# Attention in a four-stage graph and mixture kernel: row of maxima through the score banks, a division in four parts, and denominators partly summed by accumulating transfers

## The chip, the cores and the metric

One core of a Trainium2 chip. The metric is device time in microseconds of the whole kernel, launch to end, median of several runs. Times of the profile are from one execution under the hardware profiler.

## The reference

3327 tokens of width 256 go through a graph layer, a mixture of eight experts (top 2), a second graph layer, attention with 8 heads of 32 features, and a second mixture with a capacity. Each result is added to `x`. Only the attention is changed:

```python
h = _layernorm(x, ln1_g, ln1_b)
q = (h @ wq + bq).reshape(B, S, N_HEADS, dk)
...
scores = jnp.einsum('bqhd,bkhd->bhqk', q, k) / np.sqrt(dk)
attn = jax.nn.softmax(scores, axis=-1)
ctx = jnp.einsum('bhqk,bkhd->bqhd', attn, v).reshape(B, S, D)
x = x + ctx @ wo + bo
```

## The kernel before, in words

`attend` works in 26 blocks: two groups of four heads, times 13 chunks of 256 queries. A block has 26 key tiles of 128 keys, taken two at a time in 13 cycles (`CYCLES`). All engines walk the same list of cycles; the cycle within a block is `c`.

- **Scores.** For a key tile, `scores` on TensorE (PE) makes two units, each one PSUM bank of two heads (`ps_s`, three banks in rotation; a unit waits until ScalarE has taken the unit three before). The stack of queries has a row of negated maxima, so the product already has the maximum of each query subtracted. ScalarE (ACT) takes a unit with one exponential into `probs`, a ring of six key tiles.
- **Values and denominators.** `values` multiplies a tile of `probs` with the values into `ps_oz[:, 0]`. The denominator is the sum of the probabilities over all keys: `shares` multiplies by ones into `ps_oz[:, 1]`. So that PE doesn't do this for each tile, GpSimd (POOL) adds up 14 tiles of a block (`POOL_TILES`, 13 additions) into `pool_sum`, and `close` makes one set of shares of it at the start of the next block (cycle 0, after the values of tiles 24 and 25). The other 12 tiles have shares of their own. ACT may write a slot of the ring only when PE and POOL are through with it (lines 1184 to 1187).
- **Maxima.** One to two blocks ahead, `run` makes plain scores into `ps_x`, four banks in two pairs, one pair per job, two jobs per cycle; VectorE (DVE) reduces each pair to maxima (L1219, L1222). The job in pair `u % 2` waits until job `u - 2` has been taken. When a block's maxima are complete, a `row` job (cycle 9, L1148) turns them into a row, in the same pair rotation, and ACT writes that row, negated, into the query stack (L1201). At cycle 0 `close` is followed on ACT by the evacuation of `ps_oz` (L1208); at cycle 1 DVE divides (L1239, L1241); at cycle 4 an `out` job multiplies by `wo` (L1153) in the pair rotation, and DVE adds it to `x` (L1228).

The order of a cycle on PE is: both units of tile 2c, the first of tile 2c+1, the jobs, the second unit of tile 2c+1, then the values of tiles 2c-2 and 2c-1 (at cycle 0: tiles 24 and 25 of the block before, then `close`). Every engine runs its instructions in order. Plain loads are on the SP queue; POOL issues no DMA in this stage.

Of the kernel before, what the change touches and what calls it, by code (L numbers as in the profile page):

```python
# [9 lines left out]
ALU = mybir.AluOpType  # L10
# [945 lines left out]
RING = 6  # L956
POOL_TILES = [i * 23 // 13 for i in range(14)]
POOL_ADDS = len(POOL_TILES) - 1
CYCLES = NT // 2
BLOCKS = HG * NCH  # L960
MAX_AHEAD, ROW_AT, DIVIDE_AT, OUT_AT = 19, 9, 1, 4
K_PIECES = [(0, 7), (7, 14), (14, 20), (20, NT)]


def attention_jobs():


    jobs = {}
    count = 0
    full = [("max", qt, hp, kc) for kc in range(NP // KEYS) for qt in range(QT) for hp in range(2)]  # L970
    full += [("tail", 0, hp, NP // KEYS) for hp in range(2)]
    for cycle in range(-MAX_AHEAD, BLOCKS * CYCLES + OUT_AT + 1):
        now = []
        ahead, j = divmod(cycle + MAX_AHEAD, CYCLES)
        if ahead < BLOCKS:
            now += [(kind, ahead, qt, hp, kc) for kind, qt, hp, kc in full[2 * j:2 * j + 2]]
        g, c = divmod(cycle, CYCLES)
        if c == ROW_AT and 0 <= g + 1 < BLOCKS:
            now.append(("row", g + 1, 0, 0, 0))
# [4 lines left out]
    return jobs  # L984


def attend(nc, m, t, s):
# [4 lines left out]
    last_max = {job[2]: job[0] for job in flat if job[1] == "tail"}  # L992
    freed_by_act = [sum(job[1] == "row" for job in flat[:n + 1]) for n in range(len(flat))]
    UNITS = 2 * NT
    S_BANKS = 3
# [4 lines left out]
    ones_row = s("ones_row")  # L1000
    scored, exped, used = s("scored"), s("exped"), s("probs_used")
    x_made, x_free, max_made, rows_made = s("x_made"), s("x_free"), s("max_made"), s("rows_made")
    pool_added, summed, evacuated, context = s("pool_added"), s("summed"), s("evacuated"), s("context")
    with ExitStack() as ctx:
# [8 lines left out]
        probs, wo = sb("probs", [P, RING, FOUR, CHUNK]), sb("wo", [P, HG, D])  # L1013
        pool_sum = sb("pool_sum", [P, 2, FOUR, CHUNK])
        part_max, maxima = sb("part_max", [P, 2, FOUR, QT, NP // KEYS + 1]), sb("maxima", [P, FOUR * QT], BF16)
# [7 lines left out]
        def _(sp):  # L1023
# [15 lines left out]
            def load_query_stack(g):  # L1039
                hg, b = divmod(g, NCH)  # L1040
                if g >= 2:
                    sp.wait_ge(scored, (g - 1) * UNITS)
# [14 lines left out]
            for g in range(2, BLOCKS):  # L1057
# [3 lines left out]
                if g == NCH:  # L1061
                    for piece, (_, end) in enumerate(K_PIECES):
                        if piece == 2:
                            load_queries(g + 2)
                        sp.wait_ge(scored, (NCH - 1) * UNITS + 2 * end)
                        load_stack(1, piece)

        @block.gpsimd
        def _(pool):
            pool.memset(kst[STACK:STACK + 1].bitcast(F32), 1.0).then_inc(ones_row, 1)  # L1070
            for g in range(BLOCKS):
                for n, k in enumerate(POOL_TILES[1:], 1):
                    tile = g * NT + k
                    pool.wait_ge(exped, 2 * tile + 2)
                    if n == 1:
# [9 lines left out]
        def _(pe):  # L1085
            def scores(g, k, halves):
# [4 lines left out]
                for j in halves:  # L1091
                    unit = (g * NT + k) * 2 + j
                    if unit >= S_BANKS:
                        pe.wait_ge(exped, unit - S_BANKS + 1)
                    for hh in range(2):
# [10 lines left out]
            def values(g, k):  # L1106
                hg, tile = g // NCH, g * NT + k
                rows = LAST if k == NT - 1 else P
                pe.wait_ge(exped, 2 * tile + 2)
# [12 lines left out]

            def run(job):
                u, kind, g, qt, hp, kc = job
                pair = u % 2 * 2
                if u >= 2 and flat[u - 2][1] == "row":
                    pe.wait_ge(rows_made, freed_by_act[u - 2])
                elif u >= 2:
                    pe.wait_ge(x_free, u - 1 - freed_by_act[u - 2])
                if kind == "max":  # L1130
# [7 lines left out]
                elif kind == "tail":  # L1138
                    for q in range(QT):
                        for hh in range(2):  # L1140
                            at = slice((2 * hp + hh) * DK, (2 * hp + hh + 1) * DK)
                            last = pe.matmul(ps_x[:, pair + hh, q * CHUNK:q * CHUNK + NP - kc * KEYS], queries[at, g % 2, q * P:(q + 1) * P],
                                             keys[at, g // NCH, kc * KEYS:NP], start=True, stop=True)
                elif kind == "row":
                    pe.wait_ge(max_made, g + 1)
                    for h in range(FOUR):
                        for q in range(QT):
                            last = pe.matmul(ps_x[STACK:STACK + 1, pair + h // 2, h % 2 * CHUNK + q * P:h % 2 * CHUNK + (q + 1) * P],  # L1148
                                             maxima[:, h * QT + q:h * QT + q + 1], m.ident_b[:], start=True, stop=True)
                else:  # L1150
                    pe.wait_ge(context, 2 * (g + 1))
                    for q in range(QT):
                        last = pe.matmul(ps_x[:, pair + q, 0:D], cx[:, q * P:(q + 1) * P], wo[:, g // NCH, :], start=True, stop=True)  # L1153
                last.then_inc(x_made, 1)

            pe.wait_ge(ones_row, 1)
            pe.wait_ge(wo_loaded, 16)
            for cycle in sorted(jobs):
                g, c = divmod(cycle, CYCLES)
                if 0 <= g < BLOCKS:  # L1160
                    if c == 0:
                        pe.wait_ge(q_loaded[g % 2], g // 2 * 48 + 48)
                        pe.wait_ge(rows_made, g + 1)
                    scores(g, 2 * c, (0, 1))
                    scores(g, 2 * c + 1, (0,))
                for job in jobs[cycle]:
                    run(job)
                if 0 <= g < BLOCKS:
# [5 lines left out]
                elif g >= 1:  # L1174
                    values(g - 1, NT - 2)
                    values(g - 1, NT - 1)
                    close(g - 1)

        @block.scalar
        def _(act):  # L1180
            def exponentials(g, k):
                tile = g * NT + k
                if tile >= RING:
                    act.wait_ge(used, tile - RING + 1)
                    before, kb = divmod(tile - RING, NT)
                    if kb in POOL_TILES:
                        act.wait_ge(pool_added, before * POOL_ADDS + max(1, POOL_TILES.index(kb)))
                for j in range(2):
                    act.wait_ge(scored, 2 * tile + j + 1)
                    act.activation(probs[:, tile % RING, 2 * j:2 * j + 2], ps_s[:, (2 * tile + j) % S_BANKS], ACT.Exp,  # L1190
                                   scale=scale).then_inc(exped, 1)

            for cycle in sorted(jobs):
                g, c = divmod(cycle, CYCLES)
                if 0 <= g < BLOCKS:
                    exponentials(g, 2 * c)
                    exponentials(g, 2 * c + 1)
                for u, kind, block_of, *_ in jobs[cycle]:
                    if kind == "row":
                        act.wait_ge(x_made, u + 1)  # L1200
                        act.activation(qst[STACK:STACK + 1, block_of % 2, :, :].rearrange("p h n -> p (h n)"),  # L1201
                                       ps_x[STACK:STACK + 1, u % 2 * 2:u % 2 * 2 + 2, :].rearrange("p a n -> p (a n)"),
                                       ACT.Copy, scale=-1.0).then_inc(rows_made, 1)
                if g >= 1 and c == 0:
                    act.wait_ge(summed, g)
                    if g >= 2:
                        act.wait_ge(context, 2 * (g - 1))
                    act.activation(oz[:], ps_oz[:], ACT.Copy).then_inc(evacuated, 1)  # L1208

        @block.vector  # L1210
        def _(dve):
            def take(job):
# [7 lines left out]
                elif kind == "tail":  # L1220
                    both = ps_x[:, pair, :].rearrange("p a (q n) -> p a q n", q=QT)
                    dve.tensor_reduce(part_max[:, g % 2, heads, :, kc], both[:, :, :, 0:TOKENS - kc * KEYS], AX.X, ALU.max).then_inc(x_free, 1)  # L1222
                    if hp == 1:
                        dve.wait_ge(x_free, u + 1 - freed_by_act[u])
                        dve.tensor_reduce(maxima[:], part_max[:, g % 2].rearrange("p h q k -> p (h q) k"), AX.X, ALU.max).then_inc(max_made, 1)
# [4 lines left out]
            for cycle in sorted(jobs):  # L1230
                g, c = divmod(cycle, CYCLES)
                for job in jobs[cycle]:
                    if job[1] != "row":
                        take(job)
                if g >= 1 and c == DIVIDE_AT:
                    dve.wait_ge(evacuated, g)
                    if g >= 2:
                        dve.wait_ge(context, 2 * g - 2)
                    dve.reciprocal(rden[:], oz[:, 1, :]).then_inc(context, 1)  # L1239
                    dve.wait_ge(context, 2 * g - 1)  # L1240
                    dve.tensor_tensor(cx[:], oz[:, 0, :], rden[:], ALU.mult).then_inc(context, 1)  # L1241
            dve.wait_ge(x_free, len(flat) - freed_by_act[-1])

# [160 lines left out]
```

## Time and profile before

| what | us |
|---|---|
| median of 3 runs (3333.06 to 3336.5) | 3336.18 |
| the profiled execution's own time | 3331.71 |
| its span, first to last instruction | 3330.0 |
| PE busy over the span | 2526.9 (76%) |
| DVE busy | 2022.8 (61%) |
| ACT busy | 1520.0 (46%) |
| POOL busy | 1058.5 (32%) |

The attention blocks fill 1578 to 2842 us of the span. A row of a timeline merges neighbouring instructions of one line; its first number is the start, its second the stretch to the end of the last of them, and in brackets is the idle time ahead with the instruction that ended it.

### The profile page before, as it was taken

The numbers are of one execution on the slowest core, as the hardware profiler recorded it, in microseconds if no ns is written. First come the engines' busy times: TensorE is split into PE (matmuls) and PEld (weight loads), VectorE is DVE, ScalarE is ACT, GpSimd is POOL, SyncE is SP. The second block draws the span as 40 slices with busy tenths as digits, with TensorE's granted clock in tenths as the row PEclk, the third lists the DMA queues.
The fourth block names the chain that finished last, engine by engine and source line by source line (L and its number), as shares of the span: only waits on it lengthen the run. The fifth ranks groups of instructions, "written<-read, shape, count | busy, mean of one in ns | idle before, by whom it ended". The sixth has DMA issues, their size and how long they took to land. (4 is left out here: it accounts for less than half of the span.)

```text
span 3330.0 us, 54843 instructions
## 1 busy us (share of the span) xinstructions
PE 2526.9 (76%) x21272; PEld 1929.4 (58%) x21272; DVE 2022.8 (61%) x2670; ACT 1520.0 (46%) x2591; POOL 1058.5 (32%) x596
## 2 busy tenths in 40 slices
PE   0399732888891699494999999999999999317883
PEld 0388632888881588481555555555555555317883
DVE  7944522777773644545667666666666663426773
ACT  0233312666660433250656556555655556205661
POOL 0100023000005000011666666666665666230003
PEclk9999956999995899795999999999999999658997
DMA  9865204555542654254000000030000000115552
GB/s 410 360 218 175 68 33 157 213 199 210 219 172 84 239 169 161 84 163 122 9 12 14 9 14 13 14 71 12 14 9 13 14 8 6 41 41 221 208 217 99
DMA packets 140109, 375.97 MB, mean 113 GB/s; under 512 B 22032, under 2 KB 82704, under 8 KB 121872
## 3 DMA queue, kind: packets, MB, share of 16 engines
q1 hardware_dynamic: 122928, 319.82, 27.3%
q0 software_dynamic: 15696, 48.77, 4.1%
q10 hardware_dynamic: 1296, 4.75, 0.4%
q8 instruction: 132, 2.16, 0.3%
q14 instruction: 57, 0.47, 0.0%
HBM read 314.30 MB, written 58.98 MB: 112 GB/s over the span
## 5 line engine op out<-in xcount | busy, mean ns | idle before, releaser
L1219 DVE TENSOR_REDUCE at_part_max<-ps_x 128x2 f32<-128x1024 f32 x624 | 731.4, 1219 | 391.3 <-PE ps_x L1136 391.3
L1190 ACT ACTIVATE at_probs<-ps_s 128x512 f32<-128x512 f32 x1352 | 706.1, 603 | 482.0 <-PE ps_s L1096 481.3
L1082 POOL TENSOR_TENSOR at_pool_sum<-at_pool_sum,at_probs 128x1024 f32<-128x1024 f32 x312 | 746.8, 2394 | 347.0 <-ACT at_probs L1190 335.8
L1096 PE MATMUL ps_s<-at_qst,at_kst 97*128 97x256 f32 x2704 | 515.9, 314 | 5.2 <-ACT at_probs L1190 5.1
L1096 PEld LDWEIGHTS ps_s<-at_qst,at_kst 97*128 97x128 f32 x2704 | 375.3, 194 | 224.6 <-issue 128.5
L461 PE MATMUL ps_acc<-adj_hi,y_hi 128*128 128x512 f32 (+1 forms) x728 | 280.1, 385 | 230.7 <-DVE adj_lo L508 230.7
L1113 PE MATMUL ps_oz<-at_probs,k_xhat 128*32 128x256 f32 (+1 forms) x5408 | 419.7, 401 | 0.0
L508 DVE TENSOR_TENSOR adj_lo<-adj_raw,adj_hi 128x1024 fp32r<-128x1024 f32 (+1 forms) x182 | 207.4, 1147 | 241.0 <-ACT adj_hi L430 241.0
L430 ACT ACTIVATE adj_hi<-adj_raw 128x1024 fp32r<-128x1024 f32 (+1 forms) x182 | 181.9, 999 | 305.4 <-PE ps_acc L463 289.1
L732 PE MATMUL ps_ex_o<-ex_w_hi,ex_hid_hi 128*128 128x256 f32 x864 | 245.7, 284 | 75.9 <-DVE ex_hid_lo L811 69.5
L461 PEld LDWEIGHTS ps_acc<-adj_hi,y_hi 128*128 128x128 f32 x728 | 138.2, 190 | 258.8 <-issue 230.8
L462 PE MATMUL ps_acc<-adj_lo,y_hi 128*128 128x512 f32 (+1 forms) x728 | 277.1, 381 | 0.0
L463 PE MATMUL ps_acc<-adj_hi,y_lo 128*128 128x512 f32 (+1 forms) x728 | 277.1, 381 | 0.0
L781 ACT ACTIVATE ex_hid<-ps_ex_h,ex_b 128x256 f32<-128x256 f32 x432 | 197.1, 474 | 166.4 <-PE ps_ex_h L734 139.4
L830 POOL DMA_DIRECT2D results<-ex_res x54 | 38.7, 717 | 723.8 <-DVE ex_res L817 723.8
L799 DVE TENSOR_TENSOR ex_w_lo<-ex_w,ex_w_hi 128x2048 fp32r<-128x2048 f32 x108 | 242.7, 2289 | 33.8 <-ACT ex_w_hi L771 33.8
L732 PE MATMUL ps_ex_h<-ex_rt_hi,ex_w_hi 128*128 128x256 f32 x864 | 243.9, 282 | 9.8 <-DVE ex_w_lo L799 9.8
L1136 PE MATMUL ps_x<-at_keys,at_queries 32*128 32x512 f32 x1248 | 197.1, 513 | 68.1 <-DMA at_wo<-wo 40.6
L734 PE MATMUL ps_ex_h<-ex_rt_hi,ex_w_lo 128*128 128x256 f32 x864 | 241.5, 280 | 0.0
L733 PE MATMUL ps_ex_h<-ex_rt_lo,ex_w_hi 128*128 128x256 f32 x864 | 241.4, 279 | 0.0
L734 PE MATMUL ps_ex_o<-ex_w_hi,ex_hid_lo 128*128 128x256 f32 x864 | 240.4, 278 | 0.0
L733 PE MATMUL ps_ex_o<-ex_w_lo,ex_hid_hi 128*128 128x256 f32 x864 | 240.4, 278 | 0.0
(181 smaller groups left out, 3960.3 us busy)
## 6 DMA issues: line engine op xcount, KB each, us to landing
ex_w<-w SPq DMA_DIRECT2D x108, 1024.0 KB, 6.7
adj_raw<-adjT SPq DMA_DIRECT2D x156, 512.0 KB, 4.0
adj_rows<-adj SPq DMA_DIRECT2D x26, 1664.0 KB, 10.7
slots<-zeros POOLq DMA_DIRECT2D x27, 512.0 KB, 21.5
ex_rows<-slots SPq DMA_DIRECT2D x54, 256.0 KB, 2.9
results<-ex_res POOLq DMA_DIRECT2D x54, 256.0 KB, 2.7
at_qst<-qk_parts SPq DMA_DIRECT2D x78, 128.0 KB, 2.5
ex_b<-b SPq DMA_DIRECT2D x54, 128.0 KB, 2.1
```

Source lines behind the costliest of these rows:

```text
L461: pe.matmul(out, y_hi[:, k, cols], hi[:, g % PIECE_RING, at], start=k == 0, stop=False)
L462: pe.matmul(out, y_hi[:, k, cols], lo[:, g % PIECE_RING, at], start=False, stop=False)
L463: last = pe.matmul(out, y_lo[:, k, cols], hi[:, g % PIECE_RING, at], start=False, stop=k == NT - 1)
L732: pe.matmul(out, hi, by_hi, start=start, stop=False)
L733: pe.matmul(out, hi, by_lo, start=False, stop=False)
L734: return pe.matmul(out, lo, by_hi, start=False, stop=stop)
L799: dve.tensor_tensor(w_lo[:, k, layer, :], w[:, k, layer, :], w_hi[:, k, layer, :].bitcast(F32), ALU.subtract).then_inc(weights_lo, 1)
L1082: pool.tensor_tensor(pool_sum[:, g % 2], pool_sum[:, g % 2], probs[:, tile % RING], ALU.add).then_inc(pool_added, 1)
L1096: last = pe.matmul(ps_s[:, unit % S_BANKS, hh, :], kst[:, 2 * j + hh, k * P:(k + 1) * P], qst[:, g % 2, 2 * j + hh, :], start=True, stop=True)
L1113: last = pe.matmul(ps_oz[h * DK:(h + 1) * DK, 0, :], m.xhat[0:rows, k, (hg * FOUR + h) * DK:(hg * FOUR + h + 1) * DK], probs[0:rows, tile ...
L1190: act.activation(probs[:, tile % RING, 2 * j:2 * j + 2], ps_s[:, (2 * tile + j) % S_BANKS], ACT.Exp, scale=scale).then_inc(exped, 1)
L1219: dve.tensor_reduce(part_max[:, g % 2, heads, qt, kc], ps_x[:, pair, :], AX.X, ALU.max).then_inc(x_free, 1)
```

## The change

The row of maxima no longer takes a pair of `ps_x`. It takes two units of the score banks, at cycle 10, at the end of the cycle on PE; ACT writes the row in two halves. The numbers of units come from `score_units`. The `out` job moves to the end of cycle 6. The division is done in four parts of 64 queries at cycles 1 to 4. The maxima start 17 cycles ahead, not 19. Of a block's key tiles, 14 go to POOL's additions (13 as before), 8 are added into `dma_sum` by DMAs that POOL issues, each after the one before has landed (the first is a plain copy), and 4 (8, 17, 24, 25) keep shares of their own on PE. `close` makes shares of both sums.

```diff
-POOL_TILES = [i * 23 // 13 for i in range(14)]
+SUM_TILES = [k for k in range(NT - 2) if k not in (8, 17)]
+DMA_TILES = [2, 5, 9, 12, 15, 19, 21, 23]
+POOL_TILES = [k for k in SUM_TILES if k not in DMA_TILES]
-MAX_AHEAD, ROW_AT, DIVIDE_AT, OUT_AT = 19, 9, 1, 4
+MAX_AHEAD, ROW_AT, DIVIDE_AT, DIVIDE_PARTS, OUT_AT = 17, 10, 1, 4, 6
...
+            def send(g, k):
+                n, tile = DMA_TILES.index(k), g * NT + k
+                before = g * len(DMA_TILES) + n
+                pool.wait_ge(taken, tile_unit[tile] + 2)
+                if n == 0 and g >= 2:
+                    pool.wait_ge(summed, g - 1)
+                if before:
+                    pool.wait_ge(dma_added, 16 * before)
+                if n == 0:
+                    pool.dma_start(dma_sum[:, g % 2], probs[:, tile % RING]).then_inc(dma_added, 16)
+                else:
+                    pool.dma_start(dma_sum[:, g % 2], probs[:, tile % RING], accum_op=ALU.add).then_inc(dma_added, 16)
...
-                for n, k in enumerate(POOL_TILES[1:], 1):
+                for k in SUM_TILES[1:]:
+                    if k in DMA_TILES:
+                        send(g, k)
+                        continue
...
-                if k not in POOL_TILES:
+                if k not in SUM_TILES:
                     last = shares(probs[:, tile % RING], rows, False)
...
                 pe.wait_ge(pool_added, (g + 1) * POOL_ADDS)
-                shares(pool_sum[:, g % 2], P, True).then_inc(summed, 1)
+                shares(pool_sum[:, g % 2], P, False)
+                pe.wait_ge(dma_added, 16 * len(DMA_TILES) * (g + 1))
+                shares(dma_sum[:, g % 2], P, True).then_inc(summed, 1)
...
+            def row(g):
+                pe.wait_ge(max_made, g + 1)
+                for half in range(2):
+                    unit = row_unit[g] + half
+                    if unit >= S_BANKS:
+                        pe.wait_ge(taken, unit - S_BANKS + 1)
+                    for hh in range(2):
+                        for q in range(QT):
+                            col = (2 * half + hh) * QT + q
+                            last = pe.matmul(ps_s[STACK:STACK + 1, unit % S_BANKS, hh, q * P:(q + 1) * P],
+                                             maxima[:, col:col + 1], m.ident_b[:], start=True, stop=True)
+                    last.then_inc(scored, 1)
...
+                for job in jobs[cycle]:
+                    if job[1] == "out":
+                        run(job)
+                if c == ROW_AT and 0 <= g + 1 < BLOCKS:
+                    row(g + 1)
...
+                    if kb in DMA_TILES:
+                        act.wait_ge(dma_added, 16 * (before * len(DMA_TILES) + DMA_TILES.index(kb) + 1))
...
-                if g >= 1 and c == DIVIDE_AT:
+                if g >= 1 and DIVIDE_AT <= c < DIVIDE_AT + DIVIDE_PARTS:
+                    done = 2 * (DIVIDE_PARTS * (g - 1) + c - DIVIDE_AT)
+                    at = slice((c - DIVIDE_AT) * CHUNK // DIVIDE_PARTS, (c - DIVIDE_AT + 1) * CHUNK // DIVIDE_PARTS)
                     dve.wait_ge(evacuated, g)
...
+                    dve.reciprocal(rden[:, at], oz[:, 1, at]).then_inc(context, 1)
+                    dve.wait_ge(context, done + 1)
+                    dve.tensor_tensor(cx[:, at], oz[:, 0, at], rden[:, at], ALU.mult).then_inc(context, 1)
```

## Rows read from the trace of the kernel before

**Rows 1.** Windows: us from to, length, busy per engine (instructions), PEclk, DMA share, GB/s

```profile
core 0: us, PE busy (x) PEld busy (x) DVE busy (x) ACT busy (x) POOL busy (x), PEclk, DMA share, GB/s
1628.10:2842.10 1214.00, 1135.63 (x12000) 688.40 (x12000) 788.70 (x709) 713.61 (x1345) 776.27 (x325) 0.96 0.06 15
2119.80:2167.00 47.20, 44.08 (x485) 26.97 (x485) 33.43 (x30) 28.67 (x54) 31.09 (x14) 1.00 0.04 13
2069.20:2119.80 50.60, 47.39 (x485) 28.59 (x486) 33.43 (x30) 28.69 (x54) 31.04 (x14) 0.93 0.04 12
2083.00:2086.00 3.00, 3.00 (x21) 1.70 (x23) 1.07 (x2) 0.60 (x1) 0.77 (x1) 0.50 0.00 0
```

**Rows 2.** PE timeline, one block: cycles without and with shares, and three stalls

```profile
2019.24 0.61 PE L1102 MATMUL ps_oz<-at_probs,k_ones 127*32 127x256 f32 x8
2019.67 0.62 PE L1102 MATMUL ps_oz<-at_pool_sum,k_ones 128*32 128x256 f32 x8
2020.21 0.98 PE L1096 MATMUL ps_s<-at_qst,at_kst 97*128 97x256 f32 x6
...
2022.99 0.98 PE L1096 MATMUL ps_s<-at_qst,at_kst 97*128 97x256 f32 x6
...
2028.46 0.50 PE L1136 MATMUL ps_x<-at_keys,at_queries 32*128 32x512 f32 x2 [0.63 <-DVE at_part_max L1219]
...
2033.48 1.13 PE L1153 MATMUL ps_x<-at_wo,at_cx 128*128 128x256 f32 x4 [1.32 <-DVE at_part_max L1219]
2034.27 0.59 PE L1096 MATMUL ps_s<-at_qst,at_kst 97*128 97x256 f32 x2
...
2051.35 0.61 PE L1148 MATMUL ps_x<-k_ident_b,at_maxima 128*1 128x128 bf16 x8 [1.14 <-DVE at_part_max L1219]
```

**Rows 3.** DVE timeline, division of the same block and a plain cycle

```profile
2023.94 1.74 DVE L1239 RECIPROCAL at_rden<-at_oz 128x256 f32<-128x256 f32 x1
2025.71 0.42 DVE L1241 TENSOR_TENSOR at_cx<-at_oz,at_rden 128x256 f32<-128x256 f32 x1
...
2050.07 2.36 DVE L1219 TENSOR_REDUCE at_part_max<-ps_x 128x2 f32<-128x1024 f32 x2 [0.41 <-PE ps_x L1136]
```

**Rows 4.** Timeline after the last block: small divisions and products on DVE

```profile
2858.43 0.32 DVE L206 RECIPROCAL bn_rs<-bn_rs 128x26 f32<-128x26 f32 x1 [0.29 <-ACT bn_rs L270]
2858.78 0.19 DVE L207 TENSOR_TENSOR bn_nb<-bn_rs 128x26 f32<-128x26 f32 x1
```

**Rows 5.** Groups of POOL, line engine op: count, busy us, mean ns, idle before

```profile
L1082 POOL TENSOR_TENSOR at_pool_sum<-at_pool_sum,at_probs 128x1024 f32<-128x1024 f32 x312 | 746.8, 2394 | 347.0 <-ACT at_probs L1190 335.8 <-POOL at_pool_sum L1082 0.5
L830 POOL DMA_DIRECT2D results<-ex_res x54 | 38.7, 717 | 723.8 <-DVE ex_res L817 723.8
L400 POOL DMA_DIRECT2D slots<-zeros x27 | 14.6, 553 | 0.6 <-POOL zeros L393 0.6
```

**Rows 6.** POOL timeline: five additions in a row, and two DMA issues in a row

```profile
2823.26 12.45 POOL L1082 TENSOR_TENSOR at_pool_sum<-at_pool_sum,at_probs 128x1024 f32<-128x1024 f32 x5 [0.76 <-ACT at_probs L1190]
...
3287.53 0.95 POOL L849 DMA_INDIRECT got<-results,mx_get  x1 [0.30 <-issue]
3288.78 0.95 POOL L849 DMA_INDIRECT got<-results,mx_get  x1 [0.30 <-issue]
```

**Rows 7.** DMA issues: queue and count, KB each, median us from issue to landing

```profile
slots<-zeros POOLq DMA_DIRECT2D x27, 512.0 KB, 21.5
results<-ex_res POOLq DMA_DIRECT2D x54, 256.0 KB, 2.7
x_kept<-k_x SPq DMA_DIRECT2D x1, 3328.0 KB, 9.3
slots<-k_xhat,mx_put POOLq DMA_INDIRECT x78, 2.4
```

**Rows 8.** PE timeline ahead of the first block: two successive maxima jobs

```profile
1540.19 0.79 PE L1136 MATMUL ps_x<-at_keys,at_queries 32*128 32x512 f32 x2 [0.34 <-DVE at_part_max L1219]
1541.32 0.79 PE L1136 MATMUL ps_x<-at_keys,at_queries 32*128 32x512 f32 x2 [0.34 <-DVE at_part_max L1219]
```

More of the change, by code:

```diff
@@ L977, in attention_jobs @@
         g, c = divmod(cycle, CYCLES)
-        if c == ROW_AT and 0 <= g + 1 < BLOCKS:
-            now.append(("row", g + 1, 0, 0, 0))
         if c == OUT_AT and g >= 1:
@@ L984, in attention_jobs, with score_units @@
     return jobs
+def score_units():
+    tile_unit, row_unit, n = {}, {}, 0
+    for cycle in range(-CYCLES, BLOCKS * CYCLES):
+        g, c = divmod(cycle, CYCLES)
+        if g >= 0:
+            for k in (2 * c, 2 * c + 1):
+                tile_unit[g * NT + k] = n
+                n += 2
+        if c == ROW_AT and g + 1 < BLOCKS:
+            row_unit[g + 1] = n
+            n += 2
+    return tile_unit, row_unit
 def attend(nc, m, t, s):
@@ L992, in attend @@
     last_max = {job[2]: job[0] for job in flat if job[1] == "tail"}
-    freed_by_act = [sum(job[1] == "row" for job in flat[:n + 1]) for n in range(len(flat))]
-    UNITS = 2 * NT
+    tile_unit, row_unit = score_units()
     S_BANKS = 3
@@ L1000, in attend @@
     ones_row = s("ones_row")
-    scored, exped, used = s("scored"), s("exped"), s("probs_used")
-    x_made, x_free, max_made, rows_made = s("x_made"), s("x_free"), s("max_made"), s("rows_made")
+    scored, taken, used = s("scored"), s("scores_taken"), s("probs_used")
+    x_made, x_free, max_made = s("x_made"), s("x_free"), s("max_made")
+    dma_added = s("dma_added")
     pool_added, summed, evacuated, context = s("pool_added"), s("summed"), s("evacuated"), s("context")
@@ L1041, in load_query_stack @@
                 if g >= 2:
-                    sp.wait_ge(scored, (g - 1) * UNITS)
+                    sp.wait_ge(scored, tile_unit[(g - 1) * NT - 1] + 2)
                 for r, part in enumerate((0, 1, 0)):
@@ L1064, in _ @@
                             load_queries(g + 2)
-                        sp.wait_ge(scored, (NCH - 1) * UNITS + 2 * end)
+                        sp.wait_ge(scored, tile_unit[(NCH - 1) * NT + end - 1] + 2)
                         load_stack(1, piece)
@@ L1070, in _ @@
             pool.memset(kst[STACK:STACK + 1].bitcast(F32), 1.0).then_inc(ones_row, 1)
-            for g in range(BLOCKS):
-                for n, k in enumerate(POOL_TILES[1:], 1):
-                    tile = g * NT + k
-                    pool.wait_ge(exped, 2 * tile + 2)
+            def send(g, k):
[10 more added lines that the diff above has]
+                    pool.dma_start(dma_sum[:, g % 2], probs[:, tile % RING], accum_op=ALU.add).then_inc(dma_added, 16)
+            for g in range(BLOCKS):
+                for k in SUM_TILES[1:]:
+                    if k in DMA_TILES:
+                        send(g, k)
+                        continue
+                    n, tile = POOL_TILES.index(k), g * NT + k
+                    pool.wait_ge(taken, tile_unit[tile] + 2)
                     if n == 1:
@@ L1091, in scores @@
                 for j in halves:
-                    unit = (g * NT + k) * 2 + j
+                    unit = tile_unit[g * NT + k] + j
                     if unit >= S_BANKS:
-                        pe.wait_ge(exped, unit - S_BANKS + 1)
+                        pe.wait_ge(taken, unit - S_BANKS + 1)
                     for hh in range(2):
@@ L1108, in values @@
                 rows = LAST if k == NT - 1 else P
-                pe.wait_ge(exped, 2 * tile + 2)
+                pe.wait_ge(taken, tile_unit[tile] + 2)
                 if k == 0 and g:
@@ L1125, in run @@
                 pair = u % 2 * 2
[L1126 to L1129, printed above, removed]
+                if u >= 2:
+                    pe.wait_ge(x_free, u - 1)
                 if kind == "max":
@@ L1143, in run @@
                                              keys[at, g // NCH, kc * KEYS:NP], start=True, stop=True)
[L1144 to L1149, printed above, removed]
                 else:
-                    pe.wait_ge(context, 2 * (g + 1))
+                    pe.wait_ge(context, 2 * DIVIDE_PARTS * (g + 1))
                     for q in range(QT):
@@ L1162, in _ @@
                         pe.wait_ge(q_loaded[g % 2], g // 2 * 48 + 48)
-                        pe.wait_ge(rows_made, g + 1)
+                        pe.wait_ge(taken, row_unit[g] + 2)
                     scores(g, 2 * c, (0, 1))
@@ L1166, in _ @@
                 for job in jobs[cycle]:
-                    run(job)
+                    if job[1] != "out":
+                        run(job)
                 if 0 <= g < BLOCKS:
@@ L1177, in _ @@
                     close(g - 1)
+                for job in jobs[cycle]:
+                    if job[1] == "out":
+                        run(job)
+                if c == ROW_AT and 0 <= g + 1 < BLOCKS:
+                    row(g + 1)
         @block.scalar
@@ L1187, in exponentials @@
                         act.wait_ge(pool_added, before * POOL_ADDS + max(1, POOL_TILES.index(kb)))
+                    if kb in DMA_TILES:
+                        act.wait_ge(dma_added, 16 * (before * len(DMA_TILES) + DMA_TILES.index(kb) + 1))
                 for j in range(2):
-                    act.wait_ge(scored, 2 * tile + j + 1)
-                    act.activation(probs[:, tile % RING, 2 * j:2 * j + 2], ps_s[:, (2 * tile + j) % S_BANKS], ACT.Exp,
-                                   scale=scale).then_inc(exped, 1)
+                    unit = tile_unit[tile] + j
+                    act.wait_ge(scored, unit + 1)
+                    act.activation(probs[:, tile % RING, 2 * j:2 * j + 2], ps_s[:, unit % S_BANKS], ACT.Exp,
+                                   scale=scale).then_inc(taken, 1)
             for cycle in sorted(jobs):
@@ L1197, in _ @@
                     exponentials(g, 2 * c + 1)
[L1198 to L1203, printed above, removed]
+                if c == ROW_AT and 0 <= g + 1 < BLOCKS:
+                    for half in range(2):
+                        unit = row_unit[g + 1] + half
+                        act.wait_ge(scored, unit + 1)
+                        act.activation(qst[STACK:STACK + 1, (g + 1) % 2, 2 * half:2 * half + 2, :],
+                                       ps_s[STACK:STACK + 1, unit % S_BANKS], ACT.Copy, scale=-1.0).then_inc(taken, 1)
                 if g >= 1 and c == 0:
@@ L1206, in _ @@
                     if g >= 2:
-                        act.wait_ge(context, 2 * (g - 1))
+                        act.wait_ge(context, 2 * DIVIDE_PARTS * (g - 1))
                     act.activation(oz[:], ps_oz[:], ACT.Copy).then_inc(evacuated, 1)
@@ L1223, in take @@
                     if hp == 1:
-                        dve.wait_ge(x_free, u + 1 - freed_by_act[u])
+                        dve.wait_ge(x_free, u + 1)
                         dve.tensor_reduce(maxima[:], part_max[:, g % 2].rearrange("p h q k -> p (h q) k"), AX.X, ALU.max).then_inc(max_made, 1)
@@ L1232, in _ @@
                 for job in jobs[cycle]:
-                    if job[1] != "row":
-                        take(job)
-                if g >= 1 and c == DIVIDE_AT:
+                    take(job)
+                if g >= 1 and DIVIDE_AT <= c < DIVIDE_AT + DIVIDE_PARTS:
+                    done = 2 * (DIVIDE_PARTS * (g - 1) + c - DIVIDE_AT)
+                    at = slice((c - DIVIDE_AT) * CHUNK // DIVIDE_PARTS, (c - DIVIDE_AT + 1) * CHUNK // DIVIDE_PARTS)
                     dve.wait_ge(evacuated, g)
[L1237 to L1242, printed above, removed]
+                    if done:
+                        dve.wait_ge(context, done)
+                    dve.reciprocal(rden[:, at], oz[:, 1, at]).then_inc(context, 1)
+                    dve.wait_ge(context, done + 1)
+                    dve.tensor_tensor(cx[:, at], oz[:, 0, at], rden[:, at], ALU.mult).then_inc(context, 1)
+            dve.wait_ge(x_free, len(flat))
 def attention(nc, m, t, s):
```

3 lines of the change are left out of this document (2 added, 1 removed).

## The prediction, made blind

> **What bounds the kernel now.** I read the windows of the attention stage first, then one block on each engine, then what POOL and its DMAs cost elsewhere in the kernel, because the trace has no DMA on POOL in this stage. The 25 intervals between block ends take 1214 us, so 48.56 us a block [rows 1]. PE is busy 94% of that, DVE 65%, ACT 59%, POOL 64%: PE sets the pace. In the PE timeline of a block [rows 2] the reader should see two things. A cycle without shares is 2.78 us (2020.21 to 2022.99) and one set of shares is 0.43 (2019.24 to 2019.67). And three times a block PE stands still for DVE: 0.63 us after the division, 1.32 ahead of the `out` job, 1.14 ahead of the `row` job, the last two because a third job in a cycle needs a pair that DVE is still reducing. After such a stall the granted clock sometimes falls to 0.50, that is 1.2 GHz, as at 2083 us; a block without that takes 47.2 us, one with it twice 50.6, so a fall costs 1.7 us [rows 1].
>
> **PE's own work after the change.** Plain cycles: 13 x 2.78 = 36.1 us. Sets of shares: before 12 + 1 = 13, after 4 + 2 = 6, so 6 x 0.43 = 2.6 us (3.0 less). The row is 0.54 and `out` 0.79 us (2033.48 to 2034.27); both are only moved. Their stalls of 1.14 and 1.32 go: at the end of the cycle DVE has had some 2 us for the pair, and the row needs no pair. Late next would be a score bank for the row, which waits for exponentials issued over 1 us before: nothing. The `out` result is added by DVE during the next cycle's first scores, a 0.7 us piece under 0.9 us of cover; without the cover it would be a stall of up to 0.7.
>
> **The division in parts** removes little. A reciprocal of 256 columns takes 1.74 us [rows 3], one of 26 takes 0.32 [rows 4]; interpolated, 64 columns take 0.56, and the product 0.23. Four parts of 0.8 us are 3.2 us where one was 2.2. In a plain cycle DVE idles 0.41 us [rows 3], so four cycles with 0.8 each leave it 1.6 behind, less 0.4 of slack: a PE stall of about 1.2 a block (bounds 0 and 1.6), against 0.63 seen plus the hand-overs around it. I take no gain. PE and DVE by themselves would then allow 36.1 + 2.6 + 0.5 + 0.8 + 1.2 = 41.2 us a block.
>
> **POOL and its chain of DMAs** are what I expect to be late next. POOL keeps 13 additions; in a row they come every 2.49 us (12.45 / 5 [rows 6]). It gets 8 issues. Their price: the generation of a DMA of 256 KB took 0.72 us, that of the 512 KB of zeros 0.55 [rows 5]; then 0.30 until the next instruction [rows 6]. An accumulating one must also name its second source, so I take the upper, 1.02 each (bounds 0.55, as if the gap were hidden, and 1.25, the pitch of the indirect ones). Work alone is 13 x 2.49 + 8 x 1.02 = 40.5 us, as much as PE's.
>
> To that come landings. Each send waits for the one before to have landed, and it stands in POOL's queue, so the additions behind it wait as well. Call issue to landing L. Between the sends of tiles 2, 5, 9, 12, 15 and 19 lie two additions each (1.02 + 4.98 = 6.0 us), which hide an L up to 5.7. Between 19, 21 and 23 lies one, 1.02 + 2.49 = 3.5 us, so there POOL waits L + 0.3 each. After 23, `close` on PE waits for the landing, and all of the next block's tiles but 0 and 1 are queued behind it on PE, and on ACT behind the evacuation that `close` releases. POOL has only the addition of tile 1 to do meanwhile. So one block runs, from landing to landing:
> - `close`'s second shares 0.43, scores of tile 2 0.91, exponential 0.60, three hand-overs of about 0.1: 2.3 us until send 2;
> - five sends (2, 5, 9, 12, 15): 5.1 us; ten additions: 24.9 us. PE makes the 17 tiles from 2 to 19 in some 24 us, so POOL doesn't run dry;
> - sends 19, 21, 23: 3 L + 0.6.
>
> Together 32.9 + 3 L. The ring doesn't add to it: the slots of tiles 20 to 23 are asked for by tiles 0 to 3 of the next block, late in the same order.
>
> **L.** No row shows an accumulate. The nearest is the 256 KB from POOL, 2.7 us, beside 2.4 for the 128 KB of the indirect one: 0.3 per 128 KB, so 3.3 for a plain 512 KB [rows 7]. The accumulate reads 512 KB more: at (9.3 - 2.7) / (3328 - 256) us per KB, 1.1 us. That makes 4.4. Low end: 3.3, the second read for nothing. High end by the rows: 21.5, the zeros, but those were queued behind each other and large loads, so I count them as evidence for a tail only; a chain of reads and writes that don't overlap, twice the 0.6 + 1.1 of data time, gives 6.1. I take 4.4.
>
> The Trainium skill (DMA: Bandwidth & Descriptors, Anatomy of one DMA) fits a DMA from GpSimd as about 2.0 us plus bytes at 436 GB/s; by it a plain 512 KB is an estimated 3.2 us. Its page Collectives: The Full Stack (Part 3) says that a reduce is held back by its two reads and not by the addition, which would make an estimated 4.4; if the addition and second read were free, the chain below would be that of the first rival. No row here shows either.
>
> **The clock.** PE now stalls in `close` for some 5 us a block, longer than any stall of before. The mean block has (48.56 - 47.2) / 1.7 = 0.8 falls for its two long stalls [rows 1], so one follows roughly every second stall. It would lie on the chain's first piece; I take half of one, 0.85 (bounds 0 and 1.7).
>
> **The sum.** 32.9 + 13.2 + 0.85 = 46.95 us a block against 48.56: -1.6 x 26 = -42 us. Ahead of the first block, DVE paces maxima at 1.13 us a job [rows 8]; two cycles less are four jobs, -4.5. At the end the last division in four dependent parts costs +1.1. Together -45. The profiled execution took 3331.7 us (span 3330.0), 4.5 below the median; against the median, 3336.2 - 45 = 3291.
>
> **Rivals.**
> 1. The transfers are hidden, L near 3.3. The chain is 32.9 + 9.9 = 42.8, PE and DVE allow 41.2, and the freed stalls and shares show almost fully: -5.8 to -7.4 a block, -150 to -195 us, 3141 to 3186; with an issue cheaper by 0.2 the middle between this and my forecast. For it: DMA engines are 6% used in the stage [rows 1]. Against it: a dependent accumulate must read and write the same bytes. 0.25.
> 2. **Slower**: the wait in `close` and at sends 21 and 23. It decides from 32.9 + 3 L = 48.6, so L = 5.2 without a fall of the clock and 4.9 with half a one; each us of L above costs 78 us. L = 5.5 with a fall each block: 51.1, +66 us, 3399. Beyond 5.7 all seven gaps wait: L = 7 gives 2.3 + 7 x 7.3 + 7 = 60.4 us, +310. For it: POOL's own work is already 40.5 us with no landing in it, and the trace says nothing of accumulates. 0.30.
> 3. The row and `out` don't come free as they seem, since DVE after four parts of division is still behind at cycle 6; PE stalls there again by up to 1.3. Under the chain above this is hidden (POOL is the one behind); it only lifts rival 1 from 41.2 to 42.5. Within its figures.
> 4. The parts cancel: what shares and stalls give, 3.0 + 2.5 us, is eaten by the chain within 0.2%. About 0.06.
>
> **How the numbers follow.** The forecast, a chain with L between 3.7 and 4.9, has 0.39: 44.0 to 48.4 a block, 3215 to 3329. Rival 1 0.25, rival 2 0.30, no change 0.06. A measurement of this kernel tells some 0.2%, 7 us. Faster 0.64, same 0.06, slower 0.30. The range leaves out the better half of rival 1 and the far part of rival 2 (L above 5.5): 3165 to 3390.
>
> **What would show it.** Right: intervals between evacuations (L1208 before) near 47 us; POOL's idle time released by landings at tiles 21 and 23, about 1 us each; PE idle some 5 us in `close`, released by a DMA; no idle time of PE ahead of row and `out`; L of the accumulates 4 to 5 us; issues 0.7 us. Wrong: PE idle in `close` near nothing (L or the issue cheaper, rival 1); POOL waiting at all seven gaps (rival 2); DVE ending most of PE's idle time (rival 3). The steps least sure are L, which the sum multiplies by three, and the price of an issue, by five.

## The result and the profile after

The changed kernel takes 3430.5 us in the median of four runs (3398.1 to 3440.6) against 3336.1: a ratio of 1.027, with a 95% interval of 1.020 to 1.034. It is slower, by 94 us where I forecast 45 us faster, and outside my range. Its profiled execution has a span of 3424.8 us.

The first view is again the windows of the stage, here from the first evacuation of `ps_oz` to the last (us from to, length, busy time of PE, weight loads, DVE, ACT and POOL with instructions, granted clock, DMA share, GB/s); then one block in pieces.

```profile
1630.20:2934.20 1304.00, 1176.53 (x10608) 703.86 (x10608) 870.70 (x863) 719.39 (x1370) 931.04 (x524) 0.86 0.44 95
2032.40:2035.80 3.40, 0.80 (x18) 0.23 (x11) 0.43 (x1) 0.00 (x0) 2.15 (x1) 1.00 0.78 154
2038.00:2051.00 13.00, 13.00 (x78) 7.20 (x79) 10.02 (x12) 5.50 (x11) 9.62 (x6) 0.50 0.31 82
2051.00:2072.00 21.00, 21.00 (x214) 13.24 (x217) 17.77 (x18) 14.26 (x28) 18.44 (x11) 0.99 0.41 83
```

The 25 intervals are 52.16 us each, not 48.56 [rows 1] and not the 46.95 forecast. PE has 1392 matmul records less and yet more busy time: the granted clock of the stage is 0.86, where it was 0.96. The third row is what I had not reckoned with. After PE's wait of 2.6 us in `close` the clock stays at 0.50 (1.2 GHz) for 13 us, with PE busy throughout. In the kernel before, the trace has 27 stretches of low clock in the stage and each is 3.4 us long (the one of [rows 1] is among them). In the changed kernel it has 25 between the first and the last evacuation, 3.4 to 27.3 us long, and together they last 345 us, 13.8 us a block. Each of them begins in a wait of PE or at most 2.1 us after it, 23 of them at the wait in `close`.

The waits of the same stretch (engine line, waited for: us in total, times, longest):

```profile
ACT at_oz L1256 <- PE ps_oz L1134: 134.9, 26, 10.0
POOL at_dma_sum L1096 <- ACT at_probs L1238: 110.5, 25, 5.7
PE ps_oz L1134 <- DMA at_dma_sum<-at_probs: 102.6, 25, 11.1
POOL at_pool_sum L1114 <- ACT at_probs L1238: 94.2, 109, 2.1
POOL at_dma_sum L1098 <- DMA at_dma_sum<-at_probs: 81.4, 34, 7.7
POOL at_dma_sum L1098 <- ACT at_probs L1238: 66.1, 37, 4.2
PE ps_x L1168 <- DVE at_part_max L1267: 16.1, 19, 1.8
```

PE waits 102.6 / 25 = 4.1 us a block for the landing in `close`, and the waits at the `row` and `out` jobs [rows 2] are gone. But POOL, which the forecast had busy from tile 2 to tile 19, waits for ACT a further 94.2 + 66.1 us, 6.4 a block: PE at half clock delivers tiles too slowly. One block on POOL shows it:

```profile
2038.38 0.58 POOL L1096 DMA_DIRECT2D at_dma_sum<-at_probs  x1 [3.82 <-ACT at_probs L1238]
...
2044.69 0.85 POOL L1098 DMA_DIRECT2D at_dma_sum<-at_probs  x1
2047.32 4.87 POOL L1114 TENSOR_TENSOR at_pool_sum<-at_pool_sum,at_probs 128x1024 f32<-128x1024 f32 x2 [1.78 <-ACT at_probs L1238]
2053.41 0.87 POOL L1098 DMA_DIRECT2D at_dma_sum<-at_probs  x1 [1.22 <-ACT at_probs L1238]
...
2076.45 0.86 POOL L1098 DMA_DIRECT2D at_dma_sum<-at_probs  x1 [1.73 <-DMA at_dma_sum<-at_probs]
...
2081.95 0.86 POOL L1098 DMA_DIRECT2D at_dma_sum<-at_probs  x1 [2.23 <-DMA at_dma_sum<-at_probs]
```

The move of the `row` job is not quite free. The scores behind it, which otherwise take 0.98 us, take 0.53 more; the weight loads of scores wait for ACT's writes of the row (44 waits, 9.2 us, between 1640 and 2800 us).

```profile
2072.82 1.51 PE L1128 MATMUL ps_s<-at_qst,at_kst 97*128 97x256 f32 x6
```

The transfers themselves, over the whole kernel (queue, count, KB each, median us from issue to landing):

```profile
at_dma_sum<-at_probs POOLq DMA_DIRECT2D x208, 512.0 KB, 4.4
```

L is 4.4 us in the median, the value taken; for the transfer of tile 21 the median is 5.2. An issue is 0.86 us; an addition right behind it starts some 0.6 us after the issue began and takes 2.7 us where others take 2.4, so the pair is as long as both one after the other.

### The profile page after: what moved, and what is told of

The parts are those of the page before. It is cut to its first block and busy times, and to the rows that moved or that the text cites. A ratio compares the mean times of both kernels' runs of the same rounds, so it can differ in the third digit from the quotient of the medians.

```text
span 3424.8 us, 52605 instructions
## 1 busy us (share of the span) xinstructions
PE 2568.9 (75%) x19816; PEld 1946.3 (57%) x19816; DVE 2101.6 (61%) x2826; ACT 1525.3 (45%) x2617; POOL 1220.8 (36%) x804
## 5 line engine op out<-in xcount | busy, mean ns | idle before, releaser
L1114 POOL TENSOR_TENSOR at_pool_sum<-at_pool_sum,at_probs 128x1024 f32<-128x1024 f32 x312 | 768.8, 2464 | 111.5 <-ACT at_probs L1238 97.4
L1128 PE MATMUL ps_s<-at_qst,at_kst 97*128 97x256 f32 x2704 | 582.7, 341 | 6.5 <-ACT at_probs L1238 5.6
L1128 PEld LDWEIGHTS ps_s<-at_qst,at_kst 97*128 97x128 f32 x2704 | 422.2, 216 | 261.0 <-ACT at_probs L1238 137.6
L1145 PE MATMUL ps_oz<-at_probs,k_xhat 128*32 128x256 f32 (+1 forms) x5408 | 428.0, 433 | 0.7 <-ACT at_probs L1238 0.7
L1168 PE MATMUL ps_x<-at_keys,at_queries 32*128 32x512 f32 x1248 | 215.5, 568 | 68.2 <-DMA at_wo<-wo 41.1
```

Of the source, the lines that this page charges most:

```text
L1114: pool.tensor_tensor(pool_sum[:, g % 2], pool_sum[:, g % 2], probs[:, tile % RING], ALU.add).then_inc(pool_added, 1)
L1128: last = pe.matmul(ps_s[:, unit % S_BANKS, hh, :], kst[:, 2 * j + hh, k * P:(k + 1) * P], qst[:, g % 2, 2 * j + hh, :], start=True, stop=True)
```

## The experiments

**Parts alone.** The first takes the transfers out of the change:

```diff
-SUM_TILES = [k for k in range(NT - 2) if k not in (8, 17)]
-DMA_TILES = [2, 5, 9, 12, 15, 19, 21, 23]
+SUM_TILES = [i * 23 // 13 for i in range(14)]
+DMA_TILES = []
...
-                shares(pool_sum[:, g % 2], P, False)
-                pe.wait_ge(dma_added, 16 * len(DMA_TILES) * (g + 1))
-                shares(dma_sum[:, g % 2], P, True).then_inc(summed, 1)
+                shares(pool_sum[:, g % 2], P, True).then_inc(summed, 1)
```

> The change without its transfers: 14 tiles to POOL and shares of their own for 12 tiles on PE, as before; the row in the score banks, the four-part division, the later out and the 17 cycles are kept. Theory (the chain through the landings and the clock that falls after the wait in close make the change slow): PE sets the pace, 13 x 2.78 + 13 x 0.43 + 0.54 + 0.79 + up to 1.2 = 43 to 44.3 us a block at a granted clock near 1.00, so about 110 to 145 us less than before, 3190 to 3225. Rival (the moved row and the division in parts, with products on DVE that stand still beside POOL, are what costs): no faster than before, 3330 or more.

3223.7 us, ratio 0.965 (0.964 to 0.967). The block is 44.31 us at a clock of 1.00, and the first evacuation comes 4.3 us earlier than before (1623.8 against 1628.1): the two cycles less. Its window of the stage:

```profile
1623.80:2731.50 1107.70, 1102.37 (x12008) 677.83 (x12008) 837.66 (x863) 709.85 (x1369) 771.91 (x325) 1.00 0.07 17
```

The second puts the change's `send`, tile lists and two-part `close` alone into the kernel before.

> The kernel before with the transfers alone: 8 tiles by accumulating transfers, 4 by shares, 14 by POOL; row, out and division as before. Theory: the chain of POOL and landings sets the block as in the change, so 50 to 54 us a block, 3380 to 3470, with PE waiting for a landing in close 3 to 5 us a block and the clock low after it; the stalls at row and out are hidden. Rival (the transfers only hurt together with the moved row and division): the shares removed show, 3.0 us a block, 3260 to 3330.

3470.7 us, ratio 1.041 (1.035 to 1.048), a block of 53.27. The slowness is the transfers'; the rest of the change is worth 115 us without them, and 40 beside them. One part of the expectation failed: PE's waits at `row` and `out` are not hidden, they are 26.6 and 30.9 us in the stage. Only 1 of this kernel's 26 products of the division takes longer than 0.43 us, so it is slow without the second cause that is found below.

**The landing's duration.** `accum_op=ALU.add` is removed, nothing else:

> The change with all eight transfers as plain copies into dma_sum, so the denominators leave seven tiles out; each still waits for the one before. A landing then takes 2.9 us instead of 4.5 and an issue 0.58 instead of 0.86. Theory: the chain is 3 x 1.6 + 6 x 0.28 = 6.5 us shorter, the wait in close is near nothing and the clock doesn't fall: 41 to 44 us a block, 3140 to 3220. Rival (the duration of a transfer matters little, it is the order of POOL): 3400 or more.

3309.0 us, ratio 0.992 (0.990 to 0.995), a block of 47.42: 121 us faster than the change, but 3.4 us a block, 89 us in all, above what the theory allowed. The waits in `close` are nearly gone, and still the clock falls (0.94 in the stage). The waits of PE in that stage name another stall (same columns as the list of waits above):

```profile
PE ps_x L1168 <- DVE at_part_max L1267: 60.1, 72, 1.5
PE ps_oz L1134 <- DMA at_dma_sum<-at_probs: 9.9, 2, 9.5
```

**The wait filled with work.**

```diff
                 shares(pool_sum[:, g % 2], P, False)
+                for _ in range(10):
+                    shares(pool_sum[:, g % 2], P, False, nought)
                 pe.wait_ge(dma_added, 16 * len(DMA_TILES) * (g + 1))
```

> The change with ten sets of shares by weights of zero (4.3 us of products that add nothing to the sums) between the shares of pool_sum and the wait for the last landing. Theory (the 4 us wait costs mainly through the 13 us of half clock that follow it): the clock stays near 1.00, the block falls from 52.2 to 46 to 48 us, the time to 3270 to 3320, although PE has 4.3 us of work more. Rival (the landings and POOL's order alone make 52 us, whatever PE's clock): no change or longer, 3420 to 3450.

3461.5 us, ratio 1.037 (1.035 to 1.040), block 53.24: the expectation failed. The clock is low for 191 us in the stage instead of 345, so it did not stay near 1.00. It hardly falls after `close` any more; 22 of its 26 falls come some 13 us later, after another stall. In the timelines of DVE, POOL and PE of this kernel:

```profile
2052.83 0.54 DVE L1294 RECIPROCAL at_rden<-at_oz 128x64 f32<-128x64 f32 x1
2053.40 2.98 DVE L1296 TENSOR_TENSOR at_cx<-at_oz,at_rden 128x64 f32<-128x64 f32 x1
2056.30 2.34 DVE L1273 TENSOR_REDUCE at_part_max<-ps_x 128x2 f32<-128x1024 f32 x2
```

```profile
2053.02 0.85 POOL L1101 DMA_DIRECT2D at_dma_sum<-at_probs  x1
2053.62 5.15 POOL L1117 TENSOR_TENSOR at_pool_sum<-at_pool_sum,at_probs 128x1024 f32<-128x1024 f32 x2
```

```profile
2054.82 0.98 PE L1131 MATMUL ps_s<-at_qst,at_kst 97*128 97x256 f32 x6
2057.57 0.50 PE L1173 MATMUL ps_x<-at_keys,at_queries 32*128 32x512 f32 x2 [1.77 <-DVE at_part_max L1273]
2058.70 0.80 PE L1173 MATMUL ps_x<-at_keys,at_queries 32*128 32x512 f32 x2 [0.63 <-DVE at_part_max L1273]
2059.42 0.80 PE L1131 MATMUL ps_s<-at_qst,at_kst 97*128 97x256 f32 x2
```

The product of 64 columns, 0.22 us alone, takes 2.98: it ends when POOL's first addition does. A product with both operands in SBUF does not get through while POOL is adding. In the trace of the changed kernel 53 of the 104 products are held up; each of them ends 0.08 to 0.09 us after an addition does, and none of the other 51 lies wholly inside one. In the filled kernel DVE falls behind, PE stands 1.77 + 0.63 us for it, and its matmuls then take 0.80 us where they took 0.50. The filler moved the clock's fall from one stall to the next; what it saved in low clock is outweighed by its own 4.3 us a block and by PE's waits for DVE.

**The product left out, alone and with the filler.** The context is written by the reciprocal:

```diff
-                    dve.reciprocal(rden[:, at], oz[:, 1, at]).then_inc(context, 1)
-                    dve.wait_ge(context, done + 1)
-                    dve.tensor_tensor(cx[:, at], oz[:, 0, at], rden[:, at], ALU.mult).then_inc(context, 1)
+                    dve.reciprocal(cx[:, at], oz[:, 1, at]).then_inc(context, 2)
```

> The change with the four products of a block's division left out: the reciprocal alone is written to the context, so the output leaves out the multiplication by the values' sums. The wait in close stays. Theory (two causes of a low clock: the wait in close, and DVE's product held up by POOL's additions): one of two is gone, but the wait in close is still there with its 13 us of half clock; 50 to 52.5 us a block, 3375 to 3430. Rival (the products are the main cost): 46 to 48 us, 3270 to 3320.

3411.6 us, ratio 1.023 (1.020 to 1.026), block 51.45: as expected, the wait in `close` is enough by itself.

> Both at once: ten sets of shares by zero weights ahead of the wait in close, and the products of the division left out. Theory (the chain of POOL and landings costs 46 to 47 us a block once PE's clock stays up; all beyond it in the change is the clock, which falls after either stall): granted clock 0.98 or more, 46 to 47.5 us a block, 3265 to 3310. Rival (each stall costs its own length and the clock is beside the point; or POOL's order alone makes 52 us): 3400 or more, as with either alone.

3329.1 us, ratio 0.997 (0.996 to 0.998), mean block 48.36. So the filler costs 31 us alone, the missing products bring 19 alone, and both together bring 101: one stall of either kind suffices to lower the clock. The two kernels without products differ in the filler alone. With 4.3 us more work for PE in each block, the filled one is 82 us faster, at a clock of 0.98 in the stage instead of 0.87 (the wait alone, then the wait filled):

```profile
1629.20:2915.40 1286.20, 1156.12 (x10608) 695.25 (x10608) 790.69 (x763) 719.67 (x1370) 931.76 (x524) 0.87 0.45 96
1634.80:2843.90 1209.10, 1161.59 (x12608) 709.33 (x12607) 790.01 (x763) 713.70 (x1370) 934.39 (x524) 0.98 0.48 102
```

Time and mean are above what was expected; 15 of the 25 intervals are between 46.7 and 47.3. One such block, with 4.3 us of filler in it:

```profile
2009.54:2056.20 46.66, 45.85 (x509) 28.21 (x510) 33.29 (x32) 28.62 (x56) 37.43 (x21) 1.00 0.48 103
```

and its chain on POOL, where 46.66 us go by from one first send to the next:

```profile
2011.42 0.58 POOL L1099 DMA_DIRECT2D at_dma_sum<-at_probs  x1 [3.87 <-ACT at_probs L1244]
...
2039.96 0.85 POOL L1101 DMA_DIRECT2D at_dma_sum<-at_probs  x1
...
2044.98 0.86 POOL L1101 DMA_DIRECT2D at_dma_sum<-at_probs  x1 [1.77 <-ACT at_probs L1244]
...
2050.96 0.86 POOL L1101 DMA_DIRECT2D at_dma_sum<-at_probs  x1 [2.70 <-DMA at_dma_sum<-at_probs]
...
2058.08 0.58 POOL L1099 DMA_DIRECT2D at_dma_sum<-at_probs  x1 [3.87 <-ACT at_probs L1244]
```

The twelfth interval is 63.1 us; in it the second group's keys are loaded, and a landing took up to 10.5 us in this kernel. The same interval is long in the change (63.8) and with plain copies (57.9), and like the others (44.5) without transfers. That is once 10 to 16 us, which the forecast had not. Of the last five intervals, 47.5 to 54.8 us, one of 50.1 has landings of 6.4 and 6.7 us and ends in a wait of 1.9 us in `close`, and the longest, behind it, begins with 20.5 us of low clock; why those landings are late stays open.

**Plain copies and no products**, both edits above:

> All eight transfers as plain copies, and the products left out (the denominators leave out seven tiles). Theory: neither the wait in close (a landing takes 2.9 us) nor the products stall PE, the clock stays up and PE's own work shows, 41 to 42.5 us a block, 3135 to 3180. Rival (POOL's 13 additions and eight issues bound it by themselves): 45 us or more, 3240 and up.

3183.8 us, ratio 0.953 (0.952 to 0.955); 17 of 25 intervals are 41.3 to 42.0 us, beside the 41.2 that the forecast gave PE and DVE, with one of 54.0 at the keys, one of 52.1 with some 25 us of low clock in it, and a mean of 42.74. The total is just above the expected span for that. One of the short blocks:

```profile
2009.00:2050.30 41.30, 41.28 (x436) 25.67 (x432) 33.25 (x33) 28.37 (x56) 35.13 (x22) 1.00 0.31 116
```

**Fewer transfers.** Four, early, around POOL's tiles of before:

```diff
+SUM_TILES = sorted([i * 23 // 13 for i in range(14)] + [2, 6, 11, 16])
+DMA_TILES = [2, 6, 11, 16]
```

> The change without its late transfers: POOL's 14 tiles as in the kernel before, and only tiles 2, 6, 11 and 16 by transfers, three or more additions apart from the next and the last one long before close; eight tiles keep shares of their own. Theory (a transfer is harmless where its landing is waited for by nobody): PE has four sets of shares less and one more than the kernel without transfers, 3 x 0.43 = 1.3 us less a block, so 43.0 against 44.3 us, 3185 to 3200. Rival (POOL, busier by four issues, holds DVE's products longer, PE stalls for DVE and the clock falls): 3224 or more.

3295.1 us, ratio 0.987 (0.985 to 0.988), block 47.22: the rival, slower than without transfers by 71 us, though nobody waits for a landing. The products took up to 2.44 us and PE waited for DVE 71 times (43.3 us). The same kernel with the products left out:

> The kernel with transfers of tiles 2, 6, 11 and 16, with the four products of the division left out (the output leaves out that multiplication). Theory (a DVE product with both operands in SBUF stands still while POOL adds, DVE falls behind, PE stalls for it and the clock falls; four issues on POOL make that more frequent): without products PE has no stall, the clock is 1.00 and the block is 42.5 to 43.5 us instead of 47.2, 3175 to 3205. Rival (the issues or the transfers themselves slow PE or ACT): 3260 to 3300, as with the products.

3190.4 us, ratio 0.955 (0.954 to 0.957), a block of 42.90 at a clock of 1.00. So 105 us of that kernel, 4.3 a block, hang on four products of a fifth of a microsecond a block. PE's waits for DVE are 1.7 us of them, and the low clock (85 us in that stage, so half of that is lost) another 1.7; the remaining 0.9 is not accounted for.

```profile
1628.20:2700.60 1072.40, 1065.36 (x11408) 660.65 (x11408) 790.28 (x763) 707.22 (x1369) 847.96 (x425) 1.00 0.28 66
```

The division in one part, in the kernel without transfers (`DIVIDE_PARTS` 1):

> The kernel without transfers (row in the score banks, later out) with the division in one part at cycle 1, as before. Theory: the stall of 0.6 us and its hand-overs after the division come back once a block, and the clock seldom falls for it alone: 44.3 to 45.5 us a block, 3222 to 3255. Rival (four products beside POOL cost more than one, 2 us held up at worst each): faster than 3222.

3248.1 us, ratio 0.973 (0.971 to 0.974), block 45.21: four parts are worth 24 us there, more than the nothing I gave them.

**Versions that beat both.** With the division's cycles kept free of transfers:

```diff
-SUM_TILES = [k for k in range(NT - 2) if k not in (8, 17)]
-DMA_TILES = [2, 5, 9, 12, 15, 19, 21, 23]
+SUM_TILES = sorted([i * 23 // 13 for i in range(14)] + [11, 16, 20])
+DMA_TILES = [11, 16, 20]
```

> POOL's 14 tiles as in the kernel before, and transfers of tiles 11, 16 and 20 alone, after the division's cycles (tiles 2 to 9) and with landings that nobody waits for; nine tiles keep shares of their own. Theory: the products meet POOL no more than without transfers, PE saves two sets of shares, 0.9 us a block, 43.4 against 44.3 us: 3195 to 3210. Rival (any transfer on POOL costs more than the shares it saves): 3224 or more.

3209.6 us, ratio 0.962 (0.960 to 0.964), block 43.61: just inside the expected span, with 0.7 us of the 0.9 a block.

```diff
-DMA_TILES = [2, 5, 9, 12, 15, 19, 21, 23]
+DMA_TILES = [10, 13, 16, 19]
+SUM_TILES = sorted([0, 1, 3, 5, 7, 8, 11, 12, 14, 15, 17, 18, 20, 22] + DMA_TILES)
```

> Transfers of tiles 10, 13, 16 and 19, POOL's 14 tiles placed around them with two additions between transfers. Theory: three sets of shares less on PE, 1.3 us, 43.0 us a block, 3185 to 3200, if POOL, some 3.5 us late at tile 22, is through before close; otherwise, and by the rival (POOL's lateness reaches close or the next block's products), PE stalls and the clock falls: 3224 to 3300.

3207.1 us, ratio 0.961 (0.959 to 0.962), block 43.60: 7 us above the expected span. Neither version leaves anything out. The second is 131 us faster than the kernel before, measured beside it, and 223 faster than the changed one; it gets 0.7 of its 1.3 us a block. Most of that is the moved row, the later `out` and the division in parts; the transfers bring 14 to 17 us.

## Why the prediction was wrong

- **The term that failed is the clock**: "It would lie on the chain's first piece; I take half of one, 0.85 (bounds 0 and 1.7)" was the step. In the change the clock is low for 13.8 us a block, in stretches of up to 27.3 us, so PE loses an estimated 6.9 us of work a block (half of 13.8), and the loss is not on the first piece alone: POOL is starved of tiles afterwards. The chain of 46.1 us with 6.9 instead of 0.85 makes an estimated 53.0 us; measured were 52.16. With the wait filled and the products left out the kernel is 101 us faster than the change, of the 139 us between forecast and result. Of the 38 us that are left, some 16 are the one long interval and some 14 the last five; the rest is not accounted for. I had priced a long stall by the falls after short ones.
- **The bound of the products was missing.** "Four parts of 0.8 us" took the product at 0.23 us; beside POOL's additions it took 0.80 on average and up to 2.98. In the kernel before it was 0.42 us each time, but the contention was in that trace already, on the other side. In 25 of 26 blocks the product began just ahead of an addition, and it was the addition that waited: beside the product of [rows 3], which starts at 2025.71, the second of these two takes 2.63 us instead of 2.38.

```profile
2022.98 2.38 POOL L1082 TENSOR_TENSOR at_pool_sum<-at_pool_sum,at_probs 128x1024 f32<-128x1024 f32 x1 [1.72 <-ACT at_probs L1190]
2025.74 2.63 POOL L1082 TENSOR_TENSOR at_pool_sum<-at_pool_sum,at_probs 128x1024 f32<-128x1024 f32 x1 [0.37 <-ACT at_probs L1190]
```

The division in parts, over four cycles, puts products behind additions: without transfers 50 of 104 are held up too, to a mean of 0.53 us for all, but the clock never falls in that stage; with the transfers they are held longer. The Trainium skill has the rule (SBUF — State Buffer, Who interferes with whom, practical consequences): a VectorE instruction with two SBUF inputs contends with a GpSimd instruction that reads SBUF, and whichever came first keeps the other out for its whole length. The trace agrees, 2.98 us against 0.22 for the product and 2.63 against 2.38 for the addition; it was the rule against this change, and I didn't use it. This is why neither stall's removal alone showed the chain. It supplies rival 3 with a cause, and that rival was wrongly called hidden: a stall of PE is not hidden by POOL's lateness when it lowers the clock that feeds POOL. In the change itself the products are the smaller cause, 19 us.
- **The chain was right in its total, by parts that cancel.** 32.9 + 3 x 4.4 = 46.1 us against 46.66 in an undisturbed block. Of its parts in the rows of that block, send 2 to send 19 took 28.5 us (30.0 taken), 19 to 21 took 5.0 and 21 to 23 took 6.0 (4.7 each), and 23 to the next send 2 took 7.1 (6.7). L was 4.4 as taken; the issue 0.86 us with next to no gap against 1.02; PE's wait in `close` 4.1 against some 5. The start, without transfers: -4.3 against -4.5.
- **The 41.2 us for PE and DVE were luck.** They contain 1.2 us of stall for the division. But the kernel with 41.3 to 42.0 us has no products, and PE is busy in all of such a block (41.28 of 41.30 us): its own work is 41.3 us, not the 40.0 of the sum. Of the 1.3 us, 0.5 are the scores behind the row. Without transfers, too, PE's work is 44.1 us where the sum had 43.1, and the stall of 1.2 did not come: PE is idle 0.2 us a block.
- **Rival 2, slower, came in, by its place but not its condition.** It asked for L above 4.9; at L = 4.4 it had come already, because its price for the clock was the same 0.85. The estimate of 4.4 us for an accumulate that was worked out from the Trainium skill (Collectives: The Full Stack, Part 3, two reads hold it back) agrees with the 4.4 us of the trace, though no run here shows that it is the reads; the plain copy of 512 KB took 2.9 us, against the 3.2 estimated from the Trainium skill (DMA: Bandwidth & Descriptors, Anatomy of one DMA).
- **The row and `out`** gave nearly what was said: their stalls went, and came back in no run that has the move. But "nothing" for a score bank was wrong: it is 0.53 us a block.

## What to carry to other kernels

Where a change leaves TensorE one wait of 2 us or more in a loop, price it by what runs at half clock afterwards and by who is fed by that work, not by its length; and try it filled. Before work is moved to GpSimd, look for VectorE instructions with two SBUF operands that will then run beside it. In these runs a chain of dependent transfers paid only where its last landing was needed late and no send fell into the cycles with such VectorE instructions: end it several tiles ahead of its reader, and keep it out of those cycles.

## What the runs showed of the hardware

- A VectorE product of two SBUF tiles, 128 x 64, takes 0.22 us alone and as long as GpSimd's addition beside it still runs, 2.98 us at most (53 of 104 in the changed kernel, each ending 0.08 to 0.09 us after an addition). Where the product came first, in the kernel before, GpSimd's addition took 2.63 us instead of 2.38.
- After one wait of 2.6 us, TensorE ran at 0.50 for 13 us though it was busy in all of them; in that kernel such stretches were 3.4 to 27.3 us long. After 1.77 + 0.63 us in the filled kernel they were 3.4 to 10.2 us, and after waits of 0.6 to 1.3 us in the kernel before all 27 were 3.4 us.
- An accumulating transfer of 512 KB within SBUF lands 4.4 us after issue, a plain one 2.9; their issues take 0.86 and 0.58 us of GpSimd, and an addition started right behind one is 0.3 us longer than others. Beside the load of the keys a landing took 10.5 us.
